# Transformer block on one core: scores from a high and a low part in float32r, and the slots without a loop

## The reference

```
h  = layernorm(x)
q, k, v = h Wq + bq, h Wk + bk, h Wv + bv           # 16 heads of 64
p  = softmax(causal(q k^T / 8))                     # per head, 512 x 512
x1 = x + (p v) Wo + bo
g  = fp4(layernorm(x1))
y  = fp4( silu(g fp4(Wg)^T) * (g fp4(Wu)^T) )
out = x1 + y fp4(Wd)^T
```

## Time and profile before

| | |
|---|---|
| median of 3 runs | 1664.79 us (1664.41 to 1666.95) |
| the profiled execution's own time | 1665.1 us |
| its span | 1663.4 us |
| TensorE busy | 1500.7 us, 90% |
| ScalarE busy | 1139.5 us, 69% |
| VectorE busy | 1092.8 us, 66% |
| GpSimd busy | 605.2 us, 36% |
| mean granted clock | 0.974 |

### The profile page before, as it was taken

The page is one execution under the profiler, slowest core; times in us unless marked ns, Lnnn a source line. Parts: engine busy times, 40 slices in busy tenths (PEclk is TensorE's granted clock), DMA queues, the critical chain, the costliest instruction groups (busy, mean ns, idle before and its releaser), DMA issues.

```text
span 1663.4 us, 30535 instructions
## 1 busy us (share of the span) xinstructions
PE 1500.7 (90%) x9098; PEld 974.9 (59%) x9098; DVE 1092.8 (66%) x3909; ACT 1139.5 (69%) x3150; POOL 605.2 (36%) x1129
## 2 busy tenths in 40 slices
PE   4999999999899998999989999899998999999984
PEld 3656565665556665565656656556665565666653
DVE  4776667666567675676656676566765667666666
ACT  4778767677667775676756777567766667677751
POOL 2444434334243343333333433334333434334420
PEclk9999999999999999999999999999999999999996
DMA  4000000000000000000000000000000000000000
GB/s 102 1 1 1 1 10 1 11 11 11 12 1 11 11 11 12 11 1 11 11 12 11 1 11 11 12 10 4 8 11 13 10 11 1 11 4 11 5 10 13
DMA packets 34154, 17.48 MB, mean 11 GB/s; under 512 B 7512, under 2 KB 33968, under 8 KB 33968
## 3 DMA queue, kind: packets, MB, share of 16 engines
q1 hardware_dynamic: 33968, 15.24, 3.4%
HBM read 11.04 MB, written 4.19 MB: 9 GB/s over the span
## 4 chain that ended last, share of the span: by engine, by line
PE 59%; ACT 15%; DVE 13%; issue 12%; DVEq 1%; DMA 0%; POOL 0%; SPq 0%; ACTq 0%; POOLq 0%
PE bank L793 13%; PE bank L809 13%; ACT sc L403 9%; PE bank L852 9%; PE bank L941 6%; PE bank L773 4%; PE bank L775 4%; PE bank L774 3%; PE bank L930 3%; DVE sc L560 3%; ACT pT L418 2%; ACT zT L435 2%; DVE xn L747 2%; DVE ha L608 1%; DVE negmax L560 1%
## 5 line engine op out<-in xcount | busy, mean ns | idle before, releaser
L364 POOL TENSOR_SCALAR sc<-sc,rinv 128x512 f32<-128x512 f32 (+3 forms) x1024 | 553.2, 557 | 810.9 <-DVE rinv L573 807.4
L403 ACT ACTIVATE sc<-sc,negmax 128x512 f32<-128x512 f32 (+3 forms) x1024 | 566.8, 555 | 349.6 <-DVE negmax L560 347.3
L560 DVE CUSTOM_DVE_ANT_0 sc<-bank,mask 128x512 f32<-128x512 f32 (+3 forms) x1024 | 466.6, 480 | 310.1 <-PE bank L793 310.1
L809 PE MATMUL bank<-ident,sc 128*128 128x128 f32 x2560 | 361.5, 276 | 44.7 <-DVE hh L616 38.6
L809 PEld LDWEIGHTS bank<-ident,sc 128*128 128x128 f32 x2560 | 304.7, 142 | 106.4 <-DVE hh L616 45.4
L418 ACT ACTIVATE pT<-bank 128x512 f32<-128x512 f32 x512 | 301.4, 591 | 71.9 <-PE bank L809 71.7
L793 PE MATMUL bank<-k_sb,q_sb 64*128 64x512 f32 (+3 forms) x2048 | 321.1, 453 | 27.1 <-issue 25.5
L852 PE MATMUL bank<-pT,v 128*64 128x512 f32 (+3 forms) x2048 | 304.9, 440 | 0.1
L793 PEld LDWEIGHTS bank<-k_sb,q_sb 64*128 64x128 f32 x2048 | 171.0, 191 | 220.9 <-issue 187.4
L852 PEld LDWEIGHTS bank<-pT,v 128*64 128x64 f32 x2048 | 136.0, 137 | 182.9 <-issue 161.5
L403 ACT ACTIVATION_READ_ACCUMULATOR sc<-sc,negmax 128x1 f32 x1024 | 193.8, 189 | 0.0
(11 more groups left out here) (115 smaller groups left out, 1664.6 us busy)
## 6 DMA issues: line engine op xcount, KB each, us to landing
x_in<-ttn_normalized_resid_pre SPq DMA_DIRECT2D x16, 256.0 KB, 3.7
x<-ttn_normalized_resid_pre SPq DMA_DIRECT2D x16, 256.0 KB, 2.9
out_x<-y_out SPq DMA_DIRECT2D x32, 128.0 KB, 1.8
wq_in<-in_L_attn_Qs SPq DMA_DIRECT2D x1, 512.0 KB, 5.0
wk_in<-in_L_attn_Ks SPq DMA_DIRECT2D x1, 512.0 KB, 6.9
wv_in<-in_L_attn_Vs SPq DMA_DIRECT2D x1, 512.0 KB, 4.6
wo_sb<-in_L_attn_O SPq DMA_DIRECT2D x1, 512.0 KB, 5.6
wd_in<-in_L_ffn_w_down SPq DMA_DIRECT2D x1, 176.0 KB, 2.5
```

The costliest lines, as they stand in the source:

```text
L364: last = nc.gpsimd.tensor_scalar(p, p, rinv[:, h % 2, a, i:i + 1], 1.0, ALU.mult, ALU.mult)
L403: last = nc.scalar.activation(p, p, ACT.Exp, scale=-1.0, bias=negmax[:, he % 2, a, i:i + 1], accum_out=rsum[:, he % 2, a, i:i + 1])
L560: last = nc.vector.tensor_tensor_reduce(out=sc[:, h % 2, a, S_AT[i]:S_AT[i] + m], in0=bank_of(s, f"S{c}{a}")[:, at:at + m], in1=mask[:, SE ...
L809: last = nc.tensor.transpose(bank_of(s, f"P{n}")[:, dst:dst + P], sc[:, ht % 2, a, src:src + P], ident[:, :])
```

## The change

Four things change, and the diff below is cut to them.

1. q and k are kept as two float32r tensors each. ScalarE writes the high part from PSUM with the bias added (keep_high), VectorE then writes the rest, PSUM + bias - high, and frees the bank. q's high part stands on ScalarE between tanh and P0's copy, k's between the exponential of the third chunk's first half and P1's copy. VectorE's two instructions stay at their place and now wait for ScalarE's.
2. Each block of scores is three float32r products per head (high x high, high x low, low x high), the heads alternating: 24 products in a slot in place of 8.
3. The factor 1/8 of the queries moves into the weights of q, once at the start: both parts of w_q are scaled.
4. The loop is gone: all slots are written out, waits compare with constants, and the ring of banks has no unused places.

```diff
+    W_SCALE = [DH ** -0.5, 1.0, 1.0]
-    PERIOD = 2 * NPAIR
-    TURNS = NB // 2 - 2
-        q_sb = sb("q_sb", [P, 2, SEQ])
-        k_sb = sb("k_sb", [P, 2, SEQ])
+        q_hi, q_lo = sb("q_hi", [P, 2, SEQ], f32r), sb("q_lo", [P, 2, SEQ], f32r)
+        k_hi, k_lo = sb("k_hi", [P, 2, SEQ], f32r), sb("k_lo", [P, 2, SEQ], f32r)
...
-        def walk(eng, do):
-
-            for t in range(-LOAD, 0):
+        def walk(do):
+            for t in range(-LOAD, PAIRS):
                 do(Slot(t))
-            with eng.Fori(0, TURNS) as turn:
-                for t in range(PERIOD):
-                    do(Slot(t, turn))
-            for t in range(TURNS * PERIOD, PAIRS):
-                do(Slot(t))
...
+        def take_bank(kind, k, freed, until):
+
+
+            n = len(ring)
+            if n >= RING:
+                nc.tensor.wait_ge(*ring[n - RING])
+            ring.append((freed, until))
+            bank_at[kind, k] = bank[n % RING]
+            return bank[n % RING]
...
+                    if c == 0:
+                        wait(pe, q_taken, hs + 1)
+                        wait(pe, k_taken, hs + 1)
+                    to = [take_bank(f"S{c}{a}", hs, s_maxed[c][a], hs + 1) for a in range(2)]
+                    for i, at, m in S_CHUNKS[c]:
+                        for n, (q, k) in enumerate(((q_hi, k_hi), (q_hi, k_lo), (q_lo, k_hi))):
+                            for a in range(2):
+                                rows = slice(DH * a, DH * a + DH)
+                                last = nc.tensor.matmul(to[a][:, at:at + m], q[rows, hs % 2, P * i:P * i + P],
+                                                        k[rows, hs % 2, 0:m], start=(n == 0), stop=(n == 2))
+                    last.then_inc(s_done[c], 1)
...
                             nc.scalar.activation(w_hi[n][:, 512 * g:512 * g + 512].rearrange("p (h k) -> p h k", k=DH),
-                                                 w[:, NH // 2 * g:NH // 2 * (g + 1), :], ACT.Copy).then_inc(whi_set, 1)
+                                                 w[:, NH // 2 * g:NH // 2 * (g + 1), :], ACT.Copy,
+                                                 scale=W_SCALE[n]).then_inc(whi_set, 1)
...
+                def keep_high(n):
+
+                    if pj is None:
+                        return
+                    if pj == 0:
+                        act.wait_ge(b_set, 1)
+
+                    wait(act, s_done[2], pj - 1)
+                    wait(act, (q_done, k_done)[n], pj + 1)
+                    at = NPAIR * n + pj % NPAIR
+                    nc.scalar.activation((q_hi, k_hi)[n][:, pj % 2, :], bank_at["qk"[n], pj][:, :], ACT.Identity,
+                                         bias=bcol[:, at:at + 1]).then_inc((qhi_done, khi_done)[n], 1)
+
...
+                keep_high(0)
                 take_probs(0)
                 exp(2, 0)
+                keep_high(1)
                 take_probs(1)
                 exp(2, 1)
...
-                    wait(dve, s, s_done[2], pj - 1)
-                    wait(dve, s, q_done, pj + 1)
-                    nc.vector.tensor_scalar(q_sb[:, pj % 2, :], bank_of(s, "q")[:, :], DH ** -0.5, bcol[:, r:r + 1],
-                                            ALU.mult, ALU.add).then_inc(q_taken, 1)
-                    wait(dve, s, k_done, pj + 1)
-                    nc.vector.tensor_scalar(k_sb[:, pj % 2, :], bank_of(s, "k")[:, :], bcol[:, NPAIR + r:NPAIR + r + 1], None,
-                                            ALU.add).then_inc(k_taken, 1)
+                    wait(dve, qhi_done, pj + 1)
+                    nc.vector.scalar_tensor_tensor(q_lo[:, pj % 2, :], bank_at["q", pj][:, :], bcol[:, r:r + 1],
+                                                   q_hi[:, pj % 2, :].bitcast(f32), ALU.add, ALU.subtract).then_inc(q_taken, 1)
+                    wait(dve, khi_done, pj + 1)
+                    nc.vector.scalar_tensor_tensor(k_lo[:, pj % 2, :], bank_at["k", pj][:, :],
+                                                   bcol[:, NPAIR + r:NPAIR + r + 1], k_hi[:, pj % 2, :].bitcast(f32),
+                                                   ALU.add, ALU.subtract).then_inc(k_taken, 1)
```

More of the change, by code:

```diff
@@ L159, in preln_block_kernel, with __init__ @@
         class Slot:
-            def __init__(self, t, turn=None):
-                self.t, self.turn = t, turn
+            def __init__(self, t):
+                self.t = t
             def due(self, lead, limit, every=1, phase=0):
                 n = self.t + lead - phase
[L168 to L173, removed]
+                return n // every if n % every == 0 and 0 <= n // every < limit else None
             def due_duo(self, lead):
                 n = self.t + lead
-                if self.turn is not None or n < 4 * (DUOS - 2):
+                if n < 4 * (DUOS - 2):
                     return self.due(lead, DUOS, 4)
@@ L181, in due_duo @@
                 return DUOS - 2 + n if n < 2 else None
[L183 to L196, removed]
@@ L198, in wait_alone, with wait @@
[L198 to L200 removed]
+        def wait(eng, sm, k, each=1):
+            if k > 0:
+                eng.wait_ge(sm, each * k)
+        def wait_alone(eng, sm, k, each=1):
+            wait(eng, sm, k, each)
             eng.sem_inc(passed, 1)
[L203 to L205 removed]
+        def walk(do):
+            for t in range(-LOAD, PAIRS):
                 do(Slot(t))
[L207 to L211 removed]
@@ L213, in ring_users @@
[L213 to L251, removed]
@@ L255, in preln_block_kernel @@
[L255 to L264, removed]
@@ L266, in bank_of @@
[L266 to L285, removed]
@@ L288, in preln_block_kernel @@
[L288 to L292, removed]
-        block = ctx.enter_context(nc.Block())
+        ring, bank_at = [], {}
+        def take_bank(kind, k, freed, until):
[5 more added lines that the diff above has]
+            return bank[n % RING]
@@ L399, in exp @@
                         return
-                    wait(act, s, s_maxed[c][a], he + 1)
+                    wait(act, s_maxed[c][a], he + 1)
                     for i, _, m in S_CHUNKS[c]:
@@ L428, in do @@
                 if p is not None:
-                    wait(act, s, z_done, p + 1)
-                    wait(act, s, o_done, p - 1)
+                    wait(act, z_done, p + 1)
+                    wait(act, o_done, p - 1)
                     if p == 0:
@@ L568, in invert @@
                         return
-                    wait(dve, s, exp_done[c], h + 1)
+                    wait(dve, exp_done[c], h + 1)
                     lo = S_CHUNKS[c][-1][0]
@@ L584, in f1 @@
                         if fs % 2 == 0:
-                            wait(dve, s, x1_done, fs // 2 + 1, NPAIR)
+                            wait(dve, x1_done, fs // 2 + 1)
                         for j in range(2):
@@ L589, in f1 @@
                     if fa is not None:
-                        wait(dve, s, f_rstd, fa + 1, 4)
+                        wait(dve, f_rstd, fa + 1)
                         for j in range(2):
@@ L605, in swiglu @@
                     k = 2 * fu + j
-                    base = 0 if s.turn is None else s.turn * 8
-                    dve.wait_ge(tanh_done, base + k + 1)
-                    nc.vector.scalar_tensor_tensor(ha[:, j, :], th[:, j, :], 1.0, bank_of(s, f"gate{j}")[:, 0:NI], ALU.add,
+                    wait(dve, tanh_done, k + 1)
+                    nc.vector.scalar_tensor_tensor(ha[:, j, :], th[:, j, :], 1.0, bank_at["gate", k][:, 0:NI], ALU.add,
                                                    ALU.mult).then_inc(gate_taken, 1)
@@ L734, in do @@
                 if b is not None:
-                    wait(dve, s, x_loaded[b % 2], b // 2 + 1, 2 * NPAIR, 16)
+                    wait(dve, x_loaded[b % 2], b // 2 + 1, 16)
                     for j in range(NT):
@@ L743, in do @@
                 if b is not None:
-                    wait(dve, s, x_rstd, b + 1, NPAIR)
-                    wait(dve, s, xt_done, b, NPAIR)
+                    wait(dve, x_rstd, b + 1)
+                    wait(dve, xt_done, b)
                     for j in range(NT):
```

495 lines of the change are left out of this document (236 added, 259 removed).

## The result

The changed kernel takes 1746.01 us (median of 4, 1744.24 to 1748.18) against 1664.6 us for the kernel before (median of 4 here); the ratio is 1.049, with a 95% interval of 1.047 to 1.051. The forecast was 1690 with a range up to 1722: the sign was right, the size was not. The profiled execution took 1744.24 us, its span 1742.4.

What follows compares the result with a forecast made beforehand. TensorE, busy 90% of the span, was taken to bound 69 of 128 slots, waits for ScalarE or VectorE the other 59. -11 + 27 + 16 + 20 - 34 + 8 = +26 on 1665.1: about 1690, range 1646 to 1722.

Steps and rivals of the forecast that it cites:

- the clock: Granted clock falling in longer waits: +5 us in x-turned slots, +3 in gate slots, together +8 (0 to 25).
- Scores: Score products in plain slots: burst 2.19 us, 0.16 less a slot, over 69 slots -11 us.
- rival 2: Score products: the two heads don't run beside each other in float32r, 1.8 us more a slot, 1900 us; chance 0.06.
- rival 3: Plain slots: ScalarE becomes their bound too, 69 slots at about +0.35 us, +35, 1725 us; chance 0.08.
- The loop: Five jumps back written out: 25.5 us of idle and 8.5 of low clock saved, -34 us.
- The late slots: Added ScalarE work delays 29 gate, 16 down, 14 x-turned slots by 0.95, 1.0, 1.45 us: +27, +16, +20.
- Rival 1: Score burst and late slots: faster scores and lighter conversions carry the loop's gain home, 1647 us; chance 0.26.

Runs made afterwards that it cites:

- straight: The changed kernel with the split taken back (float32 q and k, no extra ScalarE work), only the loop gone: 1630.4 us, ratio 0.980.
- fill: The changed kernel with thrown-away products put ahead of TensorE's three long waits: 1697.1 us, ratio 1.021.
- split_unused: The changed kernel with float32 scores; high parts are still made and waited for, but not read for scores: 1775.4 us, ratio 1.070.
- klate: The changed kernel with VectorE's rest of k moved behind f6, the second inversion, f7 and the norm of x: 1632.9 us, ratio 0.982.

## Why the prediction was wrong

The step that failed is the clock: the prediction put +8 us on it, 3 of them in gate slots and none in down slots, and the two kinds lost 23.7 and 18.8. A second term, the first slots, was missing.

Adding up the slots of each kind, by the starts of their first score product in the traces, splits the span's 111 us from straight (1631.1) to the change (1742.4). The kinds: the first 14 slots, then 56 plain, 29 gate, 15 down and 13 with x turned. What stands ahead of the first and behind the last score start differs by 1 us.

| | before | straight | change | fill |
|---|---|---|---|---|
| first 14 | 139.6 | 139.6 | 155.9 | 154.9 |
| plain | 574.0 | 564.9 | 554.4 | 553.1 |
| gate | 419.8 | 419.9 | 470.8 | 447.1 |
| down | 222.1 | 196.4 | 230.3 | 211.5 |
| x turned | 207.3 | 209.0 | 230.8 | 227.8 |

- **Scores: right, a little low.** 64-row float32r products of two heads run beside each other, so rival 2 did not happen. The burst is 957.10 to 959.22, 2.12 us where 2.19 was worked out:

```profile
957.10 0.50 PE L232 MATMUL bank<-k_hi,q_hi 64*128 64x512 f32 x2
957.43 0.39 PE L232 MATMUL bank<-k_lo,q_hi 64*128 64x512 f32 x2
957.66 0.39 PE L232 MATMUL bank<-k_hi,q_lo 64*128 64x512 f32 x2
...
958.43 0.22 PE L232 MATMUL bank<-k_hi,q_hi 64*128 64x128 f32 x2
958.49 0.28 PE L232 MATMUL bank<-k_lo,q_hi 64*128 64x128 f32 x2
958.61 0.27 PE L232 MATMUL bank<-k_hi,q_lo 64*128 64x128 f32 x2
...
959.22 1.08 PE L289 MATMUL bank<-pT,v 128*64 128x512 f32 x4
```

  The short products of 128 columns follow each other at 0.11 to 0.12, the weight loads' pace as priced; the first follows at 0.06. Plain slots gained 10.5 us where 11 was said, though over 56 slots and not 69; ScalarE's work was hidden in them, and rival 3 did not happen.
- **The loop: right.** 33 us by the two medians, 34 foreseen.
- **The late slots: right.** With the falls taken away (fill against straight, which has none in these two kinds), gate slots cost 27.2 us more, where 27 was foreseen, and down slots 15.1 for 16. The turned x comes 11.94 us after its slot's start (1056.94 less 1045.00) against 10.47 before, 1.47 late for 1.45 foreseen.

```profile
1056.94 0.66 PE L340 MATMUL bank<-ident,xn 128*128 128x128 f32 x4 [3.87 <-DVE xn L837]
```

- **The clock: this step failed.** I put +8 us on it, with 25 as the bound: +5 in slots with x turned, at "about 1 us a fall", and +3 for "a few more falls" in gate slots. Filling the waits gave 49 us back: 23.7 in gate slots and 18.8 in down slots, kinds that had no fall before apart from those behind the loop's jumps, 3 in those with x turned, about 3 in all others. The 5 were not too small: 11 of the 13 slots with x turned have a fall in the changed kernel, and nine had one in straight already. Two errors are in the rest. The price was read off a slot with x turned, 16.47 against 15.45, while in a gate or down slot a fall costs 1.5 to 1.6 (17.3 to 15.7, 15.6 to 14.1). In that slot the down product took 0.71 us longer at the fall, but it started only 0.29 later behind the turned x (2.92 us for 2.63), though the transposes between were 0.48 slower: part of the slowing was taken up by a wait for hqT that the slot at full clock had. The two slots of the earlier trace rows, first at 1.00 and then at 0.90:

```profile
391.67 1.57 PE L930 MATMUL bank<-wdT,hqT 128*128 128x128 f32 x12 [0.45 <-ACT hqT L485]
393.08 1.02 PE L941 MATMUL bank<-zT,wo_sb 128*128 128x512 f32 x2
...
800.11 2.29 PE L930 MATMUL bank<-wdT,hqT 128*128 128x128 f32 x12
802.23 1.02 PE L941 MATMUL bank<-zT,wo_sb 128*128 128x512 f32 x2
```

  And the count was guessed as a few, though the trace had a fall behind the 2.1 us wait of the earlier trace rows in seven of these 13 slots, and the step itself made two more kinds of wait about as long: 2.38 us ahead of P2, 1.76 ahead of the down product. Of the 29 gate slots 15 then had a fall, of the 15 down slots at least 12.
- **The first slots: this term was missing.** They cost 16.3 us, of which 12 fall on seven in which VectorE quantizes a piece of the weights ahead of its row maxima, 3 us, and 4.1 on the first two. As I read the rows, k's rest, then this, then the maxima, then the exponentials now stand in a ring with ScalarE, and slots of 10.0 take 11.56. P4 waits there for the bank that q_lo frees, the last row of the waits above. The cause is only in part tried: with float32 scores these slots are as slow (157.8 us in split_unused), and with k's rest moved they take 150.8 (klate), so 5 of the 16 us are its place.

Against what was foreseen, the falls in gate and down slots (42.5 for 3) and the first slots (16.3 for nothing) make 56, and the forecast was 56 short. That they agree to the unit is chance: by slots, the two profiled executions account for 51 of it, with some us the other way in slots with x turned, and the rest is how far those executions lie from the medians.

The direction did not hang on the clock. Rival 1's rule was that the change wins if the 59 late slots lose less than 0.76 us each; the 57 in the table lost 1.87 each, and still 1.08 without the falls (27.2, 15.1 and 13 x 1.47), which is why fill, at 1697.1, is slower than the kernel before. What it left out is that these losses hang on the place of k on VectorE. Moving it takes 51 us off the split's 116 (1632.9 against 1568.3 leaves 65), and then filling the waits another 20. The 45 that are left are the split's price in that order: 11 in the first slots, 14 in gate, 15 in down and 18 in slots with x turned, less 11 in plain ones. So with k late and its waits filled the split kernel takes 1613.3, 3% under the kernel before, yet the float32 kernel with the same move takes 1568.3. Not tried: another place for ScalarE's high parts in its own queue, and the weights' quantization outside the first slots.

## What to carry to other kernels

Price a conversion by what is queued behind it on its engine and who waits there, slot by slot: 0.16 us saved in each plain slot could not pay for 1 to 1.5 us, and the falls of the clock, in the 57 others, while moving one instruction past those that others wait for gave 62 us in the kernel without the split (1630.4 to 1568.3). A wait that a change lengthens must be priced with the clock behind it, for every slot that holds it, from a slot whose later work is alike. And try each part of a change alone: here the loop's end was worth 33 us that the rest had covered.

## What the hardware showed that I had not expected

TensorE did not keep the order of products that use different rows. In heads_apart three products of one head are issued ahead of the other's, and they still start in pairs (960.78, 961.12, 961.36, two in each), at the same total time (1748.1 against 1746.0). The rows do not name the head, and that the build changed the order is not excluded; but the two of a pair start 0.010 us apart in the first pair and 0.024 in the last, against 0.004 with the heads alternating. The opening's "worked off in order" thus doesn't hold for these products. The Trainium skill (TensorE: Matmul & The Clock Gate, "The mechanism") says that products start and end strictly in program order; this trace differs, and it decides.

Thrown-away work in a wait can make a kernel faster: 8, 6 and 15 products in the three kinds of wait took 49 us off, the granted clock going from 0.950 to 0.991.
